# Head attention: how many of the sixteen heads VectorE divides by the softmax sums, fourteen instead of twelve

## The chip, the core and the metric

The kernel runs on one core of a Trainium2 chip. The core's engines are TensorE (PE; its weight loads are shown apart as PEld), VectorE (DVE), ScalarE (ACT), GpSimd (POOL) and SyncE (SP, which here only issues DMAs). Each engine works through its own queue in order and waits on semaphores for the others. The metric is the device time of one execution in microseconds; lower is better.

## The reference

```python
# first: x is (16, 512, 256), 16 heads of 16 channels
q = (x @ Wq.T + bq).reshape(B, S, H, D)
k = (x @ Wk.T + bk).reshape(B, S, H, D)
v = (x @ Wv.T + bv).reshape(B, S, H, D)
scores = jnp.einsum('bqnd,bknd->bnqk', q, k) / jnp.sqrt(jnp.float32(D))
attn = jax.nn.softmax(scores, axis=1)          # over the HEADS
out = jnp.einsum('bnqk,bknd->bnqd', attn, v)
x = layernorm(x + out @ Wo.T + bo)
# then: two layers of windowed attention (8 heads of 64) with rotary
# embedding, and a gated MLP; residual and layernorm behind them
...
```

The softmax runs over the sixteen heads, not over the keys: for each pair of query and key the sixteen scores are exponentiated and divided by their sum.

## The kernel before

The program has two stages, one after the other: `head_attention` (all sixteen sequences), and `layers`, which the change doesn't touch.

In head attention each of the 16 sequences (`n`) is cut into 16 **units** (`u`), one for each pair of a tile of 128 queries and a tile of 128 keys, four units to a query tile. A unit holds 128 x 128 scores for each of the 16 heads, 2048 columns on 128 partitions, in four PSUM banks (`S`). There is one set of these banks, so the score work of one unit follows that of the unit before. With u the unit in hand, the engines run this round, in this order in each queue:

- **TensorE**: subtract the maximum from the scores of u (L547, four matmuls, `less_max`, which waits for VectorE's `negmax`); sum the exponentials of u-2 into `Z` (L579, waits for GpSimd's `z4`); write the scores of u+1 (L537) bank by bank as ScalarE frees the banks; multiply the probabilities of u-3 by v (L564, `times_v`: its first half waits for VectorE's divide, its second half, heads 8 to 15, for GpSimd's as well); then pieces of the next sequence's projections, and in u = 3, 8, 11, 15 an output projection (L521, L523).
- **ScalarE**: four exponentials of u (L361); the logarithm of Z of u-2 and its inverse, once to SBUF (`zi`, L329, for GpSimd) and once to PSUM (`ZI`, L335, for VectorE); evacuations.
- **VectorE**: two reductions of the scores of u over the heads (L410; each waits for its half of the scores), their minimum `negmax` (L414); in u = 0, 4, 9, 12 the residual of a finished query tile (L421, `a_r`, which waits for L523); the **divide** of u-3 (L425); in u = 0, 4, 8, 12 `shift` (L433, `a_sh`, which waits for GpSimd's `rstd`); in u = 3, 7, 11, 15 the aggregation of the statistics (L440, L441, L443); in u = 2, 6, 10, 14 the statistics of one tile (L448).
- **GpSimd**: its part of the divide of u-3 (L269); two additions that bring 16 heads to 4 (L261, which waits for the exponentials of u, and L264); in u = 3, 7, 11, 15 `rstd` (L276).

The residual, statistics and `shift` belong to tiles finished up to ten units earlier, so those of u = 0, 4 and 8 are of the sequence before, and there are none of these in the first sequence. In the last sequence TensorE has no next sequence to project for.

The divide multiplies the exponentials in place by the inverse of the sum. The heads are split between two engines at `DVE_HEADS` (L144): VectorE takes heads 0 to `DVE_HEADS`-1 with `ZI` broadcast from PSUM, GpSimd the others with `zi` broadcast from SBUF.

```python
e = probs[uu % NE][:, :DVE_HEADS]                         # VectorE
nc.vector.tensor_tensor(e, e, ZI.unsqueeze(1).to_broadcast([P, DVE_HEADS, P]), ALU.mult).then_inc(s_p, 1)
...
e = probs[u % NE][:, DVE_HEADS:]                          # GpSimd
...
if part == 2 * (DVE_HEADS // JH):                         # TensorE, times_v; JH = 8
    pe.wait_ge(s_pp, UNITS * nn + uu + 1)
```

Of the kernel before, what the change touches and what calls it, by code (L numbers as in the profile page):

```python
# [47 lines left out]
def head_attention(nc, ctx, x_in, w, x_out, consts, W0=None, raw=None):  # L48
# [92 lines left out]
    QK_AT = ((1, 2), (4, 5), (6, 8), (9, 10))  # L141
    READY_AT = tuple(at[1] for at in QK_AT)
    PARTS = 3
    DVE_HEADS = 12  # L144
    PACK_AT = tuple(u + 2 for u in READY_AT)
    X_AT = 2
    LAST_LAG = 10
# [107 lines left out]
    def _(pool):  # L255
# [10 lines left out]
        def normalise(n, u):  # L266
            e = probs[u % NE][:, DVE_HEADS:]
            pool.wait_ge(s_zi, UNITS * n + u + 1)
            nc.gpsimd.tensor_tensor(e, e, zinv[u % 2][:].unsqueeze(1).to_broadcast([P, HEADS - DVE_HEADS, P]),  # L269
                                    ALU.mult).then_inc(s_pp, 1)  # L270
# [119 lines left out]
    def _(dve):  # L390
# [9 lines left out]
        def one(n, par, r):  # L400
            for u in units_of(n):
# [20 lines left out]
                if exists(nn):  # L422
                    dve.wait_ge(s_zp, UNITS * nn + uu + 1)
                    e = probs[uu % NE][:, :DVE_HEADS]
                    nc.vector.tensor_tensor(e, e, ZI.unsqueeze(1).to_broadcast([P, DVE_HEADS, P]),  # L425
                                            ALU.mult).then_inc(s_p, 1)
# [26 lines left out]
    def _(pe):  # L453
# [97 lines left out]
        def times_v(nn, uu, pn, part):  # L551
# [3 lines left out]
            if part == 0:  # L555
# [3 lines left out]
                if uu == 0:  # L559
                    pe.wait_ge(s_vv, 2 * nn + 2)  # L560
            if part == 2 * (DVE_HEADS // JH):
                pe.wait_ge(s_pp, UNITS * nn + uu + 1)
# [1062 lines left out]
def build(nc, w, y_out):  # L1625
    x_a = nc.dram_tensor("x_after_heads", (SEQS, SEQ, CH), F32).ap()
    x_b = nc.dram_tensor("x_after_layer", (SEQS, SEQ, CH), F32).ap()
    with ExitStack() as ctx:
        consts = make_constants(nc, ctx)
        W0 = load_layer(nc, ctx, 0)  # L1630
        raw = ctx.enter_context(nc.sbuf_tensor("raw_weights", [P, CT, 3 * INNER], F32))
        with ExitStack() as stage:
            head_attention(nc, stage, w["x"], w, x_a, consts, W0, raw)
        with ExitStack() as stage:
            W1 = load_layer(nc, stage, 1)
            layers(nc, stage, x_a, x_b, y_out, w, [W0, W1], raw, consts)
# [52 lines left out]
```

## Time and profile before

| | |
|---|---|
| three executions | 4153.17, 4155.80, 4156.33 us |
| median | 4155.8 us |
| the profiled execution | 4154.04 us, its span 4152.3 us |
| head attention within the span | about 0 to 1425 us |
| mean granted TensorE clock | 0.989 of full speed (2.4 GHz) |

The span is the profiled stretch from the first instruction to the last; some 1.7 us lie around it. The profile names an instruction by engine and source line. An idle time is shown in front of the instruction that ended it, with the instruction that released it. Matmuls are pipelined and their ends are modelled, so "PE busy" is not a proof that TensorE is at its limit.

### The profile page before, as it was taken

How to read it: one execution, taken by the hardware profiler on the slowest of the kernel's cores; microseconds unless marked ns; L12 is line 12 of the kernel's file. 1: busy time of each engine (PE TensorE's matmuls, PEld its weight loads, DVE VectorE, ACT ScalarE, POOL GpSimd, SP SyncE). 2: the span in 40 equal slices, each digit the busy share in tenths (PEclk: the TensorE clock that was granted, in tenths of full speed). 3: DMA queues.
4: the chain of work that ended last, by engine and by line, in shares of the span. 5: the costliest groups of instructions: out<-in, count | busy, mean ns of one | idle time of the engine just before them, and what ended most of it. 6: DMA issues, size and time to landing. Idle time of an engine off the chain costs nothing.

```text
span 4152.3 us, 95963 instructions
## 1 busy us (share of the span) xinstructions
PE 3909.4 (94%) x36004; PEld 3299.3 (79%) x36064; DVE 3028.8 (73%) x7348; ACT 2889.8 (70%) x7337; POOL 2171.2 (52%) x2168
## 2 busy tenths in 40 slices
PE   5999999999999689999999999999999999999997
PEld 3777777777777568888888888888888888888886
DVE  3888888888888666666666666666777777777775
ACT  3667777677766467777777777777777777777765
POOL 3999999999999623333333333323333333333332
PEclk8999999999999899999999999999999999999999
DMA  5453445445443100000000000000000000000000
GB/s 109 72 75 65 70 69 79 61 69 75 71 70 55 52 27 17 15 17 20 17 15 17 20 17 17 19 28 17 22 21 28 20 25 20 30 20 25 20 25 25
DMA packets 175106, 159.26 MB, mean 38 GB/s; under 512 B 22194, under 2 KB 173620, under 8 KB 174644
## 3 DMA queue, kind: packets, MB, share of 16 engines
q1 hardware_dynamic: 174644, 153.13, 19.6%
q8 instruction: 287, 4.70, 0.5%
q14 instruction: 175, 1.43, 0.1%
HBM read 52.40 MB, written 25.17 MB: 19 GB/s over the span
## 4 chain that ended last, share of the span: by engine, by line
PE 40%; ACT 11%; issue 8%; DVE 3%; POOL 3%; SPq 0%; DMA 0%; POOLq 0%; DVEq 0%; ACTq 0%
PE b_X L1452 11%; PE b_F L1521 5%; PE b_M L1574 5%; PE b_S L1472 4%; PE b_F L1600 4%; PE b_S L1482 3%; PE b_M L1493 3%; ACT L1180 2%; PE b_M L1565 2%; ACT L1186 2%; ACT b_hn L1095 1%; ACT b_g L1180 1%; ACT b_PT L1218 1%; DVE b_qT L1253 1%; DVE b_kT L1253 1%
## 5 line engine op out<-in xcount | busy, mean ns | idle before, releaser
L361 ACT ACTIVATE a_p<-a_S 128x512 f32<-128x512 f32 x1024 | 528.8, 603 | 225.4 <-PE a_S L547 225.4
L261 POOL TENSOR_TENSOR a_z<-a_p 128x1024 f32<-128x1024 f32 x256 | 604.6, 2362 | 106.7 <-ACT a_p L361 102.4
L1452 PE MATMUL b_X<-b_wqkv,b_hT 128*128 128x512 f32 x2304 | 648.4, 417 | 1.3 <-DVE b_hT L1288 1.3
L1521 PE MATMUL b_F<-b_hnT,b_w 128*128 128x256 f32 (+1 forms) x4224 | 584.9, 287 | 5.8 <-issue 5.8
L1212 ACT ACTIVATE b_p<-b_S,b_nb 128x256 f32<-128x256 f32 (+1 forms) x1024 | 444.6, 446 | 178.6 <-DVE b_nb L1264 178.5
L1521 PEld LDWEIGHTS b_F<-b_hnT,b_w 128*128 128x128 f32 (+1 forms) x4224 | 532.9, 187 | 18.5 <-issue 6.2
L1452 PEld LDWEIGHTS b_X<-b_wqkv,b_hT 128*128 128x128 f32 x2304 | 416.6, 190 | 99.8 <-issue 21.8
L989 POOL TENSOR_TENSOR b_t<-b_t 128x512 f32<-128x512 f32 x128 | 165.6, 1294 | 554.8 <-DVE b_t L1236 554.8
L425 DVE TENSOR_TENSOR a_p<-a_p,a_O 128x1536 f32<-128x1536 f32 x256 | 446.7, 1745 | 4.5 <-ACT a_O L335 4.0
L410 DVE TENSOR_REDUCE a_low_max<-a_S 128x128 f32<-128x1024 f32 x256 | 313.1, 1223 | 166.0 <-PE a_S L537 166.0
L1264 DVE CUSTOM_DVE_ANT_0 b_S<-b_S,b_mask,b_rn 128x256 f32<-128x256 f32 (+1 forms) x1024 | 399.8, 450 | 1.2 <-PE b_S L1472 1.2
L1218 ACT ACTIVATE b_PT<-b_S 128x1024 f32<-128x1024 f32 (+1 forms) x256 | 235.3, 919 | 211.9 <-PE b_S L1482 211.9
L1273 DVE TENSOR_SCALAR b_a<-b_F,w_b 128x256 f32<-128x256 f32 (+1 forms) x384 | 182.6, 476 | 269.9 <-ACT b_g L1123 269.8
L1600 PE MATMUL b_F<-w_w,b_a 128*128 128x256 f32 x1536 | 356.9, 382 | 10.3 <-DVE b_a L1273 5.4
L537 PE MATMUL a_S<-a_q,a_k 128*128 128x128 bf16 x4096 | 334.6, 221 | 20.1 <-DMA a_k<-a_parts 19.4
L547 PE MATMUL a_S<-a_nm,c_identr 128*128 128x512 f32 x1024 | 323.2, 437 | 25.7 <-DVE a_nm L414 25.4
L1053 POOL TENSOR_TENSOR b_rstd<-b_ve,c_half 128x1 f32<-128x1 f32 x128 | 69.9, 546 | 520.2 <-DVE b_ve L1365 520.2
L264 POOL TENSOR_TENSOR a_z<-a_z 128x512 f32<-128x512 f32 x256 | 330.8, 1292 | 20.1
L1037 POOL TENSOR_TENSOR b_hnT<-b_hnT 128x256 fp32r<-128x256 f32 x128 | 94.4, 737 | 448.2 <-ACT b_hnT L1086 448.2
L269 POOL TENSOR_TENSOR a_p<-a_p,a_zi 128x512 f32<-128x512 f32 x256 | 326.3, 1275 | 2.6 <-ACT a_zi L329 2.6
L579 PE MATMUL a_ZM<-a_z,c_ident 128*128 128x128 f32 x2048 | 325.4, 282 | 0.0
L1600 PEld LDWEIGHTS b_F<-w_w,b_a 128*128 128x128 f32 x1536 | 284.3, 191 | 48.4 <-DVE b_a L891 8.7
(154 smaller groups left out, 8888.0 us busy)
## 6 DMA issues: line engine op xcount, KB each, us to landing
a_q<-a_parts SPq DMA_DIRECT2D x256, 128.0 KB, 5.0
a_k<-a_parts SPq DMA_DIRECT2D x256, 128.0 KB, 5.0
a_x<-in_x SPq DMA_DIRECT2D x16, 512.0 KB, 4.0
a_xr<-in_x SPq DMA_DIRECT2D x64, 128.0 KB, 4.7
x_after_heads<-a_n SPq DMA_DIRECT2D x64, 128.0 KB, 2.7
b_x<-x_after_heads SPq DMA_DIRECT2D x16, 512.0 KB, 4.1
x_after_layer<-b_xo SPq DMA_DIRECT2D x32, 256.0 KB, 2.3
b_x<-x_after_layer SPq DMA_DIRECT2D x16, 512.0 KB, 4.1
```

What stands on the lines that cost most here:

```text
L261: nc.gpsimd.tensor_tensor(z8[:], e[:, 0:8], e[:, 8:16], ALU.add).then_inc(s_zt, 1)
L264: nc.gpsimd.tensor_tensor(z4[u % 4][:], z8[:, 0:4], z8[:, 4:8], ALU.add).then_inc(s_zt, 1)
L269: nc.gpsimd.tensor_tensor(e, e, zinv[u % 2][:].unsqueeze(1).to_broadcast([P, HEADS - DVE_HEADS, P]), ALU.mult).then_inc(s_pp, 1)
L361: nc.scalar.activation(probs[u % NE][:, hs], S[:, hs], ACT.Exp, scale=HDIM ** -0.5).then_inc(s_exp, 1)
L425: nc.vector.tensor_tensor(e, e, ZI.unsqueeze(1).to_broadcast([P, DVE_HEADS, P]), ALU.mult).then_inc(s_p, 1)
L537: last = nc.tensor.matmul(S[:, h], k8[:, h % JH, h // JH, kt * P:(kt + 1) * P], q8[:, h % JH, h // JH, qt * P:(qt + 1) * P], start=(h % 4 ...
L579: last = nc.tensor.matmul(Z, ident[:], z4[uu % 4][:, j], start=(j == 0), stop=(j == 3), skip_group_check=True)
L1212: last = nc.scalar.activation(probs[hf][:, i, keys(w_)], SB[:, i, keys(w_)], ACT.Exp, bias=nb[hf][:, i:i + 1], scale=-1.0, accum_out=rs[w_ ...
L1264: last = nc.vector.tensor_tensor_reduce(out=SB[:, i, cols], in0=SB[:, i, cols], in1=hidden_keys, scale=rn[w_ % 2][:, h:h + 1], scalar=LARG ...
L1452: last = nc.tensor.matmul(X[i][:], hT_of(k, a), wqkv[:, b, k, i * INNER:(i + 1) * INNER], start=(k == 0 and (a, b) == PART_PAIRS[0]), stop ...
L1521: last = nc.tensor.matmul(F[i % 2][0:size, part], w1[:, a, k, col:col + size], hnT[:, b, k, hf * 2 * P:(hf + 1) * 2 * P], start=(k == 0 an ...
L1600: last = nc.tensor.matmul(F[1][:, t], a_sb[h][:, c, t * P:(t + 1) * P], W[layer(-d)]["w2"][:, c], start=(c == 0), stop=(c == CHUNKS - 1))
```

## The change

`DVE_HEADS` goes from 12 to 14. VectorE's divide (L425) then covers 14 x 128 = 1792 columns instead of 1536, and GpSimd's (L269) 2 x 128 = 256 instead of 512, in each of the 256 units. No instruction is added, removed or moved, on any engine. TensorE's wait for GpSimd stays at the same place in `times_v`, since 12 // 8 and 14 // 8 are both 1. Buffers, DMAs and matmuls are the same.

```diff
     READY_AT = tuple(at[1] for at in QK_AT)
     PARTS = 3
-    DVE_HEADS = 12
+    DVE_HEADS = 14
     PACK_AT = tuple(u + 2 for u in READY_AT)
```

## Rows read from the trace of the kernel before

**Rows 1.** Busy by stretch: length, then busy us (instructions) per engine, clock, DMA
```profile
core 0: us, PE busy (x) PEld busy (x) DVE busy (x) ACT busy (x) POOL busy (x), PEclk, DMA share, GB/s
...
600.00:900.00 300.00, 293.21 (x3636) 235.31 (x3652) 261.19 (x315) 211.12 (x490) 284.48 (x185) 1.00 0.48 73
```

**Rows 2.** Waits from 600 to 1400 us: us in total, times, longest
```profile
DVE a_low_max L410 <- PE a_S L537: 67.0, 115, 1.5
PEld a_S L547 <- DVE a_nm L414: 57.5, 96, 1.3
...
POOL a_z L261 <- ACT a_p L361: 25.2, 53, 1.1
...
DVE a_sh L433 <- POOL a_rs L276: 4.6, 10, 0.5
```

**Rows 3.** Groups of instructions, 600 to 1400 us: busy, mean ns | idle before
```profile
L425 DVE TENSOR_TENSOR a_p<-a_p,a_O 128x1536 f32<-128x1536 f32 x152 | 265.2, 1745 | 0.3
...
L269 POOL TENSOR_TENSOR a_p<-a_p,a_zi 128x512 f32<-128x512 f32 x152 | 193.8, 1275 | 0.0
...
L421 DVE TENSOR_TENSOR a_r<-a_B,a_xr 128x256 f32<-128x256 f32 x38 | 16.2, 425 | 23.5 <-PE a_B L523 23.5
```

**Rows 4.** The page's groups: GpSimd's 256-column two-input operation
```profile
L1037 POOL TENSOR_TENSOR b_hnT<-b_hnT 128x256 fp32r<-128x256 f32 x128 | 94.4, 737 | 448.2 <-ACT b_hnT L1086 448.2
```

**Rows 5.** Timeline, unit 2 and the start of 3: start, length, instruction [idle before]
```profile
596.75 1.74 DVE L425 TENSOR_TENSOR a_p<-a_p,a_O 128x1536 f32<-128x1536 f32 x1
596.88 0.76 PEld L547 LDWEIGHTS a_S<-a_nm,c_identr 128*128 128x128 f32 x4 [0.66 <-DVE a_nm L414]
...
598.41 0.42 DVE L448 BATCH_NORM_STATS2 a_stats<-a_r 128x6 f32<-128x256 f32 x1
...
599.15 1.23 DVE L410 TENSOR_REDUCE a_low_max<-a_S 128x128 f32<-128x1024 f32 x1 [0.32 <-PE a_S L537]
```

**Rows 6.** Timeline, unit 8 (a shift, no residual)
```profile
606.79 1.74 DVE L425 TENSOR_TENSOR a_p<-a_p,a_O 128x1536 f32<-128x1536 f32 x1
606.92 0.77 PEld L547 LDWEIGHTS a_S<-a_nm,c_identr 128*128 128x128 f32 x4 [0.94 <-DVE a_nm L414]
...
608.99 0.21 DVE L433 TENSOR_SCALAR a_sh<-a_mv,a_rs 128x1 f32<-128x1 f32 x1 [0.46 <-POOL a_rs L276]
...
609.20 1.23 DVE L410 TENSOR_REDUCE a_low_max<-a_S 128x128 f32<-128x1024 f32 x1
```

**Rows 7.** Timeline, units 0 and 1 (residual, divide and shift in unit 0)
```profile
650.09 0.88 PEld L547 LDWEIGHTS a_S<-a_nm,c_identr 128*128 128x128 f32 x4
...
650.50 0.42 DVE L421 TENSOR_TENSOR a_r<-a_B,a_xr 128x256 f32<-128x256 f32 x1 [0.47 <-PE a_B L523]
650.84 1.75 DVE L425 TENSOR_TENSOR a_p<-a_p,a_O 128x1536 f32<-128x1536 f32 x1
...
652.51 0.21 DVE L433 TENSOR_SCALAR a_sh<-a_mv,a_rs 128x1 f32<-128x1 f32 x1
...
652.63 1.22 DVE L410 TENSOR_REDUCE a_low_max<-a_S 128x128 f32<-128x1024 f32 x1
...
653.25 0.81 PEld L564 LDWEIGHTS a_O<-a_p,a_v 128*32 128x32 f32 x32
...
655.02 0.29 DVE L414 TENSOR_TENSOR a_nm<-a_ZM,a_low_max 128x128 fp32r<-128x128 f32 x1
...
655.36 0.76 PEld L547 LDWEIGHTS a_S<-a_nm,c_identr 128*128 128x128 f32 x4 [0.25 <-DVE a_nm L414]
```

**Rows 8.** Timeline, units 4, 5: subtraction, reduction without idle time, next subtraction
```profile
670.95 0.87 PEld L547 LDWEIGHTS a_S<-a_nm,c_identr 128*128 128x128 f32 x4
...
673.49 1.22 DVE L410 TENSOR_REDUCE a_low_max<-a_S 128x128 f32<-128x1024 f32 x1
...
676.23 0.77 PEld L547 LDWEIGHTS a_S<-a_nm,c_identr 128*128 128x128 f32 x4 [0.60 <-DVE a_nm L414]
```

**Rows 9.** Timeline, units 12 and 13
```profile
633.34 0.29 DVE L414 TENSOR_TENSOR a_nm<-a_ZM,a_low_max 128x128 fp32r<-128x128 f32 x1
...
633.86 0.86 PEld L547 LDWEIGHTS a_S<-a_nm,c_identr 128*128 128x128 f32 x4
```

**Rows 10.** Timeline, unit 10 of the last sequence, and the drain behind unit 15
```profile
1373.88 1.22 DVE L410 TENSOR_REDUCE a_low_max<-a_S 128x128 f32<-128x1024 f32 x1
...
1376.61 0.76 PEld L547 LDWEIGHTS a_S<-a_nm,c_identr 128*128 128x128 f32 x4 [1.18 <-DVE a_nm L414]
...
1410.25 0.63 PEld L564 LDWEIGHTS a_O<-a_p,a_v 128*32 128x32 f32 x16 [1.03 <-POOL a_p L269]
...
1413.53 0.81 PEld L564 LDWEIGHTS a_O<-a_p,a_v 128*32 128x32 f32 x32 [0.48 <-DVE a_p L425]
...
1416.80 1.35 PEld L564 LDWEIGHTS a_O<-a_p,a_v 128*32 128x32 f32 x32 [2.46 <-DVE a_p L425]
```

## The prediction

> **What bounds the kernel now.** I read the busy time by stretch first. In head attention TensorE is busy 293.2 of 300 us, GpSimd 284.5, VectorE 261.2 [rows 1]. Three engines are near full, so busy shares don't say which one sets the pace, and I went on to the waits. There the reader sees a ring of two: VectorE's reductions wait for TensorE's scores 115 times, and TensorE's subtraction waits for VectorE's negmax 96 times in the same 800 us [rows 2]. Nothing on TensorE or ScalarE waits for GpSimd in that stretch: it is named as a releaser once only, of VectorE's `shift`, 10 times, 4.6 us in all. GpSimd itself is released by the exponentials 53 times [rows 2]. So GpSimd is busy beside the ring, not in it.
>
> The ring is: subtraction (L547), exponentials, scores of the next unit (L537), two reductions and a minimum on VectorE, and the next subtraction. From one subtraction to the next reduction an undisturbed unit takes 599.15 - 596.88 = 2.27 us [rows 5], and from the reduction to the next subtraction 655.36 - 652.63 = 2.73 us [rows 7]. VectorE's divide lies in the first of these legs, beside TensorE and ScalarE. It costs nothing as long as VectorE is back before the scores are there. The question is therefore, unit by unit, how much room VectorE has left before its first reduction.
>
> **The size of the edit.** VectorE's divide takes 1745 ns for 1536 columns, and its 256-column operation with one operand in PSUM 425 ns [rows 3]. The slope is (1745 - 425) / 1280 = 1.031 ns a column, so 256 more columns cost 0.264 us. The bound above is the plain share, 1745 x 256/1536 = 291 ns, which counts the fixed part twice. I take 0.264, since both rows are of the same engine, type and kind of operands; the lower bound is the same number. Over 256 units that is 68 us more VectorE busy time. GpSimd's divide falls from 1275 ns to about 737, which is what its 256-column operation takes in the second stage [rows 3, 4]: 0.54 us a unit, 138 us less busy time.
>
> **Where GpSimd's 0.54 us goes.** TensorE doesn't wait for it in steady state [rows 2], so the gain is zero there. In unit 8 VectorE's `shift` waits 0.46 us for GpSimd's rstd [rows 6]. Yet the reduction behind it starts 609.20 - 606.92 = 2.28 us after the subtraction, as in the undisturbed unit: that wait was filling room. With the longer divide it shrinks to about 0.2 us and the reduction stays where it is.
>
> **Where VectorE's 0.264 us goes**, by kind of unit:
> - *Units with statistics or aggregation* (eight of sixteen). The tightest has 0.32 us idle before its reduction [rows 5], which covers 0.264 with 0.06 left. Cost zero. If the divide grew by more than 0.32 us, that cover would be gone.
> - *Plain units, and unit 9*, have more room than those, except in the last sequence. Cost zero.
> - *Units 0, 4 and 12*, where the residual stands ahead of the divide and `shift` behind it. The residual starts when TensorE's output is there. Then residual, divide, shift and reduction follow without a gap: the reduction shows no idle time, and stands 652.63 - 650.09 = 2.54 us after the subtraction [rows 7], and 673.49 - 670.95 = 2.54 [rows 8]. That is 0.27 us later than 2.27. VectorE is already late here, so all of the 0.264 us is added to the reduction, and to the negmax.
> - *Who pays for that.* Behind unit 0 TensorE waits 0.25 us for the negmax [rows 7], behind unit 4 0.60 us [rows 8]: the whole delay passes on, and as every engine's next work hangs on that subtraction, nothing gives it back later. Behind unit 12 TensorE is busy with the projection of v. Its subtraction starts at 633.86 without an idle time, while the negmax ended at 633.63 [rows 9]; elsewhere the load follows the end of the negmax by 0.05 us (655.31 to 655.36 [rows 7]). So 0.18 us is covered, and 0 to 0.08 us is left to pay; I take 0.02, since the modelled ends of the projection hide some more room.
> - *The divide's own reader*, `times_v`, starts at 653.25 while the divide ended at 652.59 [rows 7]; 0.66 us covers 0.264.
>
> **The sum.** Units 0 and 4 have a residual in 15 sequences (not in the first): 30 x 0.264 = 7.92 us. In the last sequence TensorE projects nothing ahead, so units 12 and 9 count in full: in unit 9 the reduction also comes without idle time, and TensorE waits 1.18 us behind it [rows 10]. 2 x 0.264 = 0.53 us. Unit 12 of the other 15: 15 x 0.02 = 0.3 us (bounds 0 and 1.2). In the drain one product waits 1.03 us for GpSimd's divide, which is 0.54 us shorter, and the next two wait for VectorE's, each 0.264 longer [rows 10]: -0.54 + 0.53, nothing. Together 7.92 + 0.53 + 0.3 = 8.75 us. The second stage is untouched. On the profiled execution's 4154.04 us this gives 4162.8; that execution lies 1.8 us under the median of the three, and on the median 4155.8 it gives 4164.5 us, 0.21% slower. With the bounds of the terms the sum runs from 8.4 to 32 x 0.291 + 15 x 0.11 = 11.0 us, so 4164.2 to 4166.8.
>
> **Rivals.**
> 1. *The delay is hidden after all: 4155.8.* TensorE's busy share of 98% [rows 1] may mean that it is the pacer, the waits before L547 being ones in which earlier matmuls still drain; then 0.264 us of later negmax costs nothing. For it: the idle before the subtraction behind unit 0 is only 0.25 us [rows 7], about the delay itself. Against it: the start follows the negmax by 0.05 us, behind units 0 and 4 alike, although their other work differs.
> 2. *The cover of the statistics units fails: about 4178, slower.* The place is the 0.32 us before the reduction [rows 5]; it decides from a divide 0.32 us longer. At 0.40 us it would cost 32 x 0.40 = 12.8, the 15 units 12 another 15 x 0.22 = 3.3, and some 63 statistics units 0.08 each and 63 with aggregation a little less, 7: +23 us. Against it: even the proportional price is 0.291.
> 3. *GpSimd is in the path after all: faster, about 4147.* It is busy 95% of the time and loses 0.54 us a unit. The whole stage's waits put down to it would have to go: 17 waits for rstd like the 0.46 us one [rows 6], nearly 8 us, and a little over 1 us in the drain [rows 10], together 9 us, while rival 1 also holds so that the longer divide is free. Against it: unit 8's reduction is on time as it is. The Trainium skill, GPSIMD Engine Reference, section Engine selection, says that elementwise work on a tile belongs on VectorE and that GpSimd is about twice as slow for two inputs. The prices here agree (GpSimd (1275 - 737) / 256 = 2.1 ns a column, VectorE 1.03), and by that rule the change gives back 138 us for 68 and should be faster. It says which engine does a column cheaper, not which has room in the ring.
>
> **The numbers.** My forecast (0.2 to 0.27% slower) gets 0.71, rival 1 gets 0.17, rival 2 gets 0.06, rival 3 gets 0.06. About 0.2% (8.3 us) is what a measurement of this kernel can tell from no change, and the forecast stands almost on that line: of its 0.71 I count 0.44 above and 0.27 below. So slower 0.44 + 0.06 = 0.50, same 0.27 + 0.17 = 0.44, faster 0.06. The range 4154 to 4168 takes in the forecast with its bounds and rival 1; it leaves out rivals 2 and 3. The forecast's own range is 4162 to 4168, with the scatter of the runs.
>
> **What would show it.** In the changed kernel's profile L425 should take 2.01 us and L269 0.74. In units 0 and 4 the reduction should start 2.80 us after the subtraction instead of 2.54, and the round of sixteen units should grow by 0.53 us or a little more. The statistics units should keep about 0.06 us of idle time before L410, and `shift` in unit 8 should wait about 0.2 us. The first reduction should come without idle time in no more kinds of unit than now. GpSimd should wait for the exponentials in nearly every unit. I am wrong if L425 grows by more than 0.32 us, if TensorE's subtraction behind unit 0 keeps its place in the round, or if the round gets shorter.

## The result, and the profile after

| | median | executions |
|---|---|---|
| before | 4157.6 us | 12 |
| changed | 4166.1 us | 12 |
| ratio | 1.0021, 95% interval 1.0012 to 1.0030 | |

The changed kernel is 8.4 us slower, and the interval lies above 1. 4164.5 us was forecast, 8.7 us above the median known then; the median of before has since risen by 1.8 us with nine more executions.

The groups of instructions from 600 to 1400 us (busy, mean ns | idle before), which answer to [rows 3]:

```profile
L425 DVE TENSOR_TENSOR a_p<-a_p,a_O 128x1792 f32<-128x1792 f32 x151 | 303.6, 2011 | 0.3
...
L269 POOL TENSOR_TENSOR a_p<-a_p,a_zi 128x256 f32<-128x256 f32 x151 | 110.7, 733 | 0.0
```

VectorE's divide grew by 2011 - 1745 = 266 ns, GpSimd's fell by 542 ns. The waits of the same stretch, against [rows 2]:

```profile
POOL a_z L261 <- ACT a_p L361: 113.2, 142, 1.7
...
PEld a_S L547 <- DVE a_nm L414: 60.7, 95, 1.6
...
DVE a_low_max L410 <- PE a_S L537: 29.3, 56, 1.2
...
DVE a_sh L433 <- POOL a_rs L276: 1.9, 10, 0.2
```

GpSimd now waits for the exponentials in 142 of some 151 units, 113 us instead of 25: its saved time became idle time. VectorE's room before the first reduction fell from 67 to 29 us. TensorE waits for VectorE 3 us more. The timeline of units 0 and 1 (sequence 2, counted from 0) shows where, against [rows 7]:

```profile
231.09 0.87 PEld L547 LDWEIGHTS a_S<-a_nm,c_identr 128*128 128x128 f32 x4
...
231.84 2.01 DVE L425 TENSOR_TENSOR a_p<-a_p,a_O 128x1792 f32<-128x1792 f32 x1
...
233.77 0.21 DVE L433 TENSOR_SCALAR a_sh<-a_mv,a_rs 128x1 f32<-128x1 f32 x1
...
233.89 1.22 DVE L410 TENSOR_REDUCE a_low_max<-a_S 128x128 f32<-128x1024 f32 x1
...
236.63 0.77 PEld L547 LDWEIGHTS a_S<-a_nm,c_identr 128*128 128x128 f32 x4 [0.52 <-DVE a_nm L414]
```

From the subtraction to the reduction it takes 2.80 us (2.54 before), and TensorE's idle time behind it is 0.52 us instead of 0.25. The same point of the round comes again here:

```profile
318.78 1.22 DVE L410 TENSOR_REDUCE a_low_max<-a_S 128x128 f32<-128x1024 f32 x1
```

The round of sixteen units takes 318.78 - 233.89 = 84.89 us. In the same sequence of the kernel before it took 314.95 - 230.60 = 84.35:

```profile
230.60 1.22 DVE L410 TENSOR_REDUCE a_low_max<-a_S 128x128 f32<-128x1024 f32 x1
...
314.95 1.22 DVE L410 TENSOR_REDUCE a_low_max<-a_S 128x128 f32<-128x1024 f32 x1
```

TensorE's idle time behind unit 4 grew as well, from 0.60 us [rows 8] to 0.86:

```profile
257.75 0.77 PEld L547 LDWEIGHTS a_S<-a_nm,c_identr 128*128 128x128 f32 x4 [0.86 <-DVE a_nm L414]
```

A unit with statistics, against [rows 5]:

```profile
262.77 0.76 PEld L547 LDWEIGHTS a_S<-a_nm,c_identr 128*128 128x128 f32 x4 [0.66 <-DVE a_nm L414]
...
264.56 0.42 DVE L448 BATCH_NORM_STATS2 a_stats<-a_r 128x6 f32<-128x256 f32 x1
...
265.04 1.23 DVE L410 TENSOR_REDUCE a_low_max<-a_S 128x128 f32<-128x1024 f32 x1
```

The reduction still comes 2.27 us after the subtraction. The statistics end at 264.98, so 0.06 us of idle time is left, too little for the view to print.

Whole profiles differ in their start and in the second stage as well, so I compare the head attention stage by itself: from its first reduction to TensorE's first operation of the second stage. Of before, and below it of the changed kernel:

```profile
56.90 1.23 DVE L410 TENSOR_REDUCE a_low_max<-a_S 128x128 f32<-128x1024 f32 x1 [45.03 <-PE a_S L537]
...
1438.38 0.66 PE L1430 MATMUL b_X<-c_ident,b_x 128*128 128x128 f32 x2 [16.82 <-DMA b_x<-x_after_heads]
```

```profile
59.38 1.23 DVE L410 TENSOR_REDUCE a_low_max<-a_S 128x128 f32<-128x1024 f32 x1 [48.03 <-PE a_S L537]
...
1449.35 0.66 PE L1430 MATMUL b_X<-c_ident,b_x 128*128 128x128 f32 x2 [17.00 <-DMA b_x<-x_after_heads]
```

The stage took 1381.5 us before and 1390.0 us after: +8.5. The granted clock was 1.00 in both kernels from 600 to 1400 us. The other 3.5 us between the two spans are 2.5 us of a later first reduction and 1.0 us in the second stage, which the change doesn't touch.

### The profile page after: what moved, and what is told of

It reads as the page before. It is cut to its first block, busy times and chain, and to the rows that moved or that the text cites. A ratio compares the mean times of both kernels' runs of the same rounds, so it can differ in the third digit from the quotient of the medians.

```text
span 4164.3 us, 96023 instructions
## 1 busy us (share of the span) xinstructions
PE 3924.2 (94%) x36064; PEld 3298.5 (79%) x36064; DVE 3097.3 (74%) x7348; ACT 2886.9 (69%) x7337; POOL 2032.7 (49%) x2168
## 4 chain that ended last, share of the span: by engine, by line
PE 40%; ACT 11%; issue 8%; DVE 3%; POOL 3%; SPq 0%; DMA 0%; POOLq 0%; DVEq 0%; ACTq 0%
PE b_X L1452 11%; PE b_F L1521 5%; PE b_M L1574 5%; PE b_S L1472 4%; PE b_F L1600 4%; PE b_S L1482 3%; PE b_M L1493 3%; ACT L1180 2%; PE b_M L1565 2%; ACT L1186 2%; ACT b_hn L1095 1%; ACT b_g L1180 1%; ACT b_PT L1218 1%; DVE b_qT L1253 1%; DVE b_kT L1253 1%
## 5 line engine op out<-in xcount | busy, mean ns | idle before, releaser
L425 DVE TENSOR_TENSOR a_p<-a_p,a_O 128x1792 f32<-128x1792 f32 x256 | 514.8, 2011 | 3.6 <-ACT a_O L335 3.0
L410 DVE TENSOR_REDUCE a_low_max<-a_S 128x128 f32<-128x1024 f32 x256 | 313.1, 1223 | 114.3 <-PE a_S L537 106.6
L537 PEld LDWEIGHTS a_S<-a_q,a_k 128*128 128x128 bf16 x4096 | 274.7, 98 | 50.1 <-issue 22.8
L410 DVE TENSOR_REDUCE a_ZM<-a_S 128x128 f32<-128x1024 f32 x256 | 313.1, 1223 | 0.0
```

Source lines behind the costliest of these rows:

```text
L410: nc.vector.tensor_reduce(out=(low_max[:], HIGH_MAX)[half], in_=S[:, 8 * half:8 * half + 8].rearrange("p h q -> p q h"), axis=AX.X, op=ALU ...
L537: last = nc.tensor.matmul(S[:, h], k8[:, h % JH, h // JH, kt * P:(kt + 1) * P], q8[:, h % JH, h // JH, qt * P:(qt + 1) * P], start=(h % 4 ...
```

## The experiments

Each kernel ran against the kernel before on the same chip, eleven executions of most, twelve of the changed kernel, five of heads15 and heads11. "Stage" is the stretch just described, read from the one profile of each kernel, against 1381.5 us before. The ratio of a call is not the quotient of the two medians beside it; the two differ by up to 0.06%.

| kernel | median us | before, same call | ratio (95%) | stage us | stage against before |
|---|---|---|---|---|---|
| changed (14 heads) | 4166.1 | 4157.6 | 1.0021 (1.0012 to 1.0030) | 1390.0 | +8.5 |
| late14 | 4166.3 | 4157.0 | 1.0023 (1.0014 to 1.0032) | 1390.3 | +8.8 |
| rest14 | 4157.8 | 4157.0 | 1.0000 (0.9992 to 1.0009) | 1381.6 | +0.2 |
| swap12 | 4154.6 | 4157.0 | 0.9992 (0.9983 to 1.0001) | 1378.6 | -2.9 |
| swap14 | 4153.8 | 4157.0 | 0.9998 (0.9989 to 1.0006) | 1377.3 | -4.2 |
| heads13 | 4160.1 | 4156.7 | 1.0006 (0.9997 to 1.0015) | 1385.7 | +4.2 |
| heads15 | 4170.0 | 4156.7 | 1.0032 (1.0019 to 1.0045) | 1395.9 | +14.4 |
| heads11 | 4180.5 | 4156.7 | 1.0057 (1.0044 to 1.0069) | 1405.3 | +23.9 |
| pool_short | 4155.3 | 4156.7 | 0.9999 (0.9990 to 1.0008) | 1380.4 | -1.0 |

### Where the two heads cost: late14 and rest14

`uu` is the unit that is divided, three behind the unit in hand. late14 takes fourteen heads in the divides that run in units 0, 4, 9 and 12, rest14 in all others.

```diff
+    def dve_heads(uu):
+        return 14 if (uu + 3) % UNITS in (0, 4, 9, 12) else 12   # rest14: 12 ... else 14
...
-            e = probs[u % NE][:, DVE_HEADS:]
+            e = probs[u % NE][:, dve_heads(u):]
...
-                    e = probs[uu % NE][:, :DVE_HEADS]
+                    e = probs[uu % NE][:, :dve_heads(uu)]
```

> VectorE takes fourteen heads only in the divides that it runs in units 0, 4, 9 and 12 (behind a residual), twelve in all others: 64 of 256 divides. The ring theory (the longer divide costs only where VectorE is already late for its first reduction) expects the whole loss: 32 late reductions of 0.267 us, +8.5 us on before, about 4166. A theory of load (the price goes with the columns moved) expects a quarter of the 8.4 us, +2.1. A theory by which GpSimd's shorter divide or its traffic matters everywhere expects also about a quarter.

> The mirror image: fourteen heads in the 192 divides of the other units, twelve in units 0, 4, 9 and 12. The ring theory expects no change against before (0, within 1 us), since the statistics units' 0.32 us of room covers 0.27. The load theory expects three quarters of the loss, +6.3. If that cover were not real, each of 126 statistics and aggregation units would add something here.

A quarter of the longer divides brought the whole loss (+8.8 us in the stage), the other three quarters none (+0.2). The theory of load (the price goes with the columns moved), which expected +2.1 and +6.3, falls with both. Timelines of late14 (above) and rest14 (below), units 0 and 1 (lines are five higher here: L552 is the subtraction, L415 the reduction, L430 the divide):

```profile
226.97 0.88 PEld L552 LDWEIGHTS a_S<-a_nm,c_identr 128*128 128x128 f32 x4
...
227.73 2.01 DVE L430 TENSOR_TENSOR a_p<-a_p,a_O 128x1792 f32<-128x1792 f32 x1
...
229.78 1.21 DVE L415 TENSOR_REDUCE a_low_max<-a_S 128x128 f32<-128x1024 f32 x1
...
234.78 1.23 DVE L415 TENSOR_REDUCE a_low_max<-a_S 128x128 f32<-128x1024 f32 x1 [0.66 <-PE a_S L542]
```

```profile
224.35 0.86 PEld L552 LDWEIGHTS a_S<-a_nm,c_identr 128*128 128x128 f32 x4
...
225.11 1.74 DVE L430 TENSOR_TENSOR a_p<-a_p,a_O 128x1536 f32<-128x1536 f32 x1
...
226.90 1.22 DVE L415 TENSOR_REDUCE a_low_max<-a_S 128x128 f32<-128x1024 f32 x1
...
229.49 2.01 DVE L430 TENSOR_TENSOR a_p<-a_p,a_O 128x1792 f32<-128x1792 f32 x1
...
231.90 1.23 DVE L415 TENSOR_REDUCE a_low_max<-a_S 128x128 f32<-128x1024 f32 x1 [0.40 <-PE a_S L542]
```

In late14 the reduction comes 2.81 us after the subtraction, in rest14 2.55 as before. In rest14's unit 1 the long divide takes its 0.27 us out of VectorE's idle time, 0.40 us against the 0.66 us that late14's unit 1, with the short divide, still has.

### Taking the lateness away: swap12 and swap14

VectorE runs the divide first and the residual, which has to wait for TensorE's output, behind it:

```diff
-                if written_out(n, u, 1):
-                    ...
-                    nc.vector.tensor_tensor(resid[qt % 2][:], Y[qt], x_res[qt % 2][:], ALU.add).then_inc(s_r, 1)
                 if exists(nn):
                     dve.wait_ge(s_zp, UNITS * nn + uu + 1)
...
                                             ALU.mult).then_inc(s_p, 1)
+                if written_out(n, u, 1):
+                    ...
+                    nc.vector.tensor_tensor(resid[qt % 2][:], Y[qt], x_res[qt % 2][:], ALU.add).then_inc(s_r, 1)
```

> Twelve heads as before, but VectorE runs the divide first and the residual (which waits for TensorE's output) behind it. In units 0 and 4 the reduction should come 2.27 us after the subtraction instead of 2.54; behind unit 0 TensorE then stops waiting (0.25 us gained), behind unit 4 it gains 0.27, behind unit 12 nothing, as the projection of v hides it; in the last sequence units 9 and 12 give 0.15 and 0.27. Ring theory: 15 x 0.25 + 15 x 0.27 + 0.4 = -8.2 us on before, about 4149.5. If TensorE's own work were the pacer (the delay hidden), it expects 0.

> The same order (divide ahead of the residual) with fourteen heads. From the start of the divide at 649.95 VectorE would need 1.93 + 0.34 + 0.12 us and be ready for the reduction at about 652.34, where 652.36 is on time. Ring theory: the two heads cost nothing any more, same as swap12 within 1.5 us, about -8 us on before. If the two heads cost by their load, it is 8.4 us above swap12.

The main part of the second expectation held: with the divide first, fourteen heads cost nothing against twelve (stage 1377.3 and 1378.6 us). The round of sixteen units takes 84.17 us in both (in swap14 from 231.99 to 316.16); 1.2 of the 1.3 us between the two stages lie behind the last sequence's reduction of unit 15's scores. There TensorE waits for GpSimd's divide 0.54 and 2.19 us in swap12, and 1.83 us in swap14, whose divide on GpSimd is shorter. The same two heads cost 8.5 us in one order and none in the other. The first expectation missed, and with it the level of the second: swap12 gained 2.9 us in the stage, not 8.2, and swap14 4.2 us, not about 8. The intervals of both ratios reach past 1, so neither is shown to beat the kernel before. Both do beat the changed kernel: their intervals end at 1.0001 and 1.0006, its own begins at 1.0012. The timeline of swap12, units 4 and 5, has the reason (L419 is the divide here, L426 the residual):

```profile
250.71 0.87 PEld L547 LDWEIGHTS a_S<-a_nm,c_identr 128*128 128x128 f32 x4
251.41 2.06 ACT L361 ACTIVATE a_p<-a_S 128x512 f32<-128x512 f32 x4 [0.88 <-PE a_S L547]
...
253.08 1.23 DVE L410 TENSOR_REDUCE a_low_max<-a_S 128x128 f32<-128x1024 f32 x1 [0.22 <-PE a_S L537]
...
255.08 1.13 PE L480 MATMUL a_B<-a_xT,a_wq 128*128 128x512 f32 x2
...
255.82 0.87 PEld L547 LDWEIGHTS a_S<-a_nm,c_identr 128*128 128x128 f32 x4 [0.44 <-DVE a_nm L414]
256.53 2.06 ACT L361 ACTIVATE a_p<-a_S 128x512 f32<-128x512 f32 x4 [0.42 <-PE a_S L547]
```

First, VectorE is ready and waits 0.22 us for the scores, and they come 2.37 us after the subtraction, not 2.27: in unit 4, whose subtraction stands right behind TensorE's output projection, the exponentials begin 0.70 us after the weight load, where behind other units it is 0.59 (before: 259.20 to 259.80 in unit 6, but 248.92 to 249.62 in unit 4). VectorE was late by 0.17 us, not by 0.27. Second, an earlier negmax is of little use behind unit 4: TensorE's projection (L480) streams until 256.21, past the load at 255.82, and the exponentials again begin 0.71 us behind the load. From unit 4's subtraction to unit 6's it takes 10.24 us (250.71 to 260.95), hardly less than before (248.92 to 259.20, 10.28). The round took 316.54 - 232.37 = 84.17 us:

```profile
232.37 1.22 DVE L410 TENSOR_REDUCE a_low_max<-a_S 128x128 f32<-128x1024 f32 x1
...
316.54 1.23 DVE L410 TENSOR_REDUCE a_low_max<-a_S 128x128 f32<-128x1024 f32 x1
```

That is 0.18 us less than before, 2.7 us in fifteen rounds.

### The dose: heads13 and heads15

```diff
-    DVE_HEADS = 12
+    DVE_HEADS = 13      # heads15: 15
```

> Thirteen heads on VectorE, three on GpSimd. The ring theory expects half of what fourteen cost, 32 x 0.133 = +4.3 us on before, with the round of sixteen units 0.27 us longer (84.35 to 84.62).

> Fifteen heads on VectorE, one on GpSimd: a divide 0.40 us longer than before. If only the late units pay: 32 x 0.40 = 12.8, and 15 units 12 in which 0.28 of the 0.40 is covered, 1.8, so +13 to +15 us. If the 0.32 us of the statistics units were all the room there is (rival 2's point of decision), 63 of them add 0.08 each and 63 aggregation units 0.03, +20 to +22. Successive VectorE instructions overlap by about 0.08 us, which speaks for the first.

The stage gave +4.2, +8.5 and +14.4 us for one, two and three heads. The round of heads13 took 84.63 us (231.08 to 315.71), where 84.62 was expected. For thirteen heads the whole-kernel ratio alone could not tell the loss from none; the stage could. heads15 kept the theory's first branch. Its timeline (unit 6):

```profile
687.12 2.14 DVE L425 TENSOR_TENSOR a_p<-a_p,a_O 128x1920 f32<-128x1920 f32 x1
687.26 0.76 PEld L547 LDWEIGHTS a_S<-a_nm,c_identr 128*128 128x128 f32 x4 [0.66 <-DVE a_nm L414]
...
689.18 0.42 DVE L448 BATCH_NORM_STATS2 a_stats<-a_r 128x6 f32<-128x256 f32 x1
689.53 1.22 DVE L410 TENSOR_REDUCE a_low_max<-a_S 128x128 f32<-128x1024 f32 x1
```

This is a statistics unit. The divide is 0.40 us longer than at twelve heads, more than the 0.32 us of printed idle time, yet the reduction is on time (2.27 us after the load). It starts 0.07 us before the statistics end: VectorE begins an instruction before the last one is through, so its room is larger than the idle time printed.

### GpSimd: pool_short and heads11

pool_short leaves out part of the computation: heads 12 and 13 stay undivided.

```diff
-            e = probs[u % NE][:, DVE_HEADS:]
+            e = probs[u % NE][:, DVE_HEADS + 2:]        # pool_short
...
-    DVE_HEADS = 12
+    DVE_HEADS = 11                                      # heads11
```

> GpSimd's side of the change alone: VectorE divides twelve heads as before, GpSimd only heads 14 and 15, so that heads 12 and 13 stay undivided (this part of the computation is left out). The ring theory expects no change (0 within 1 us). If GpSimd were in the path (rival 3), the time would fall by up to 9 us.

> The other direction: eleven heads on VectorE, five on GpSimd, whose divide grows from 1.27 to about 1.54 us. VectorE's lateness alone would give a gain of a few us at most. But GpSimd's queue then needs, start to start, 2.44 + 1.25 + 1.54 us a unit and four times 0.51 for rstd, 85.7 us a round, against the 84.35 us that the round takes. So GpSimd should become the pacer: +1.4 us a round, +15 to +22 us in all, and TensorE should wait for GpSimd's divide. If GpSimd could never be the bound, the result is -4 to 0.

Cutting GpSimd's divide in half without touching VectorE's did next to nothing: ratio 0.9999, stage -1.0 us. VectorE's divide took 1744 ns in it, as before (1745), so GpSimd's shorter work doesn't speed VectorE's either. Rival 3 falls. Of the 1.0 us, 0.8 lies behind the last sequence's reduction of unit 15's scores (from there to the second stage 1399.08 to 1437.47, before 1399.21 to 1438.38). There TensorE does wait for GpSimd's divide; the wait of 1.03 us [rows 10] became this one:

```profile
1409.57 0.38 PEld L564 LDWEIGHTS a_O<-a_p,a_v 128*32 128x32 f32 x16 [0.82 <-POOL a_p L269]
```

But GpSimd was near: one head more on it cost 23.9 us in the stage, a little more than the 15 to 22 us that the length of its queue said. The timeline of heads11 shows the wait that twelve heads don't have:

```profile
676.57 2.38 POOL L261 TENSOR_TENSOR a_z<-a_p 128x1024 f32<-128x1024 f32 x1
...
679.03 1.27 POOL L264 TENSOR_TENSOR a_z<-a_z 128x512 f32<-128x512 f32 x1
...
680.26 1.55 POOL L269 TENSOR_TENSOR a_p<-a_p,a_zi 128x640 f32<-128x640 f32 x1
...
681.77 2.36 POOL L261 TENSOR_TENSOR a_z<-a_p 128x1024 f32<-128x1024 f32 x1
...
681.86 0.38 PEld L564 LDWEIGHTS a_O<-a_p,a_v 128*32 128x32 f32 x16 [0.35 <-POOL a_p L269]
```

GpSimd runs here with no gap above 0.08 us, 5.20 us from one addition to the next, and TensorE's second half of the product with v waits for its divide. The round of sixteen units took 85.81 us (235.70 to 321.51), where 85.7 was expected from the queue's length. GpSimd's late rstd holds VectorE too: in unit 8 of heads11 `shift` waits 1.32 us, and the reduction comes 2.92 us after the subtraction (275.09 to 278.01) instead of 2.27. How the 23.9 us divide between the two waits I didn't take apart.

## Why the prediction was right, step by step

- **The size of the edit.** 0.264 us was forecast from a 256-column operation of the same engine, 0.266 measured. GpSimd 0.737 forecast, 0.733 measured.
- **Which units pay.** late14 and rest14 show that the whole loss lies in units 0, 4, 9 and 12. The timelines divide it: units 0 and 4 in every round, which grew by 0.54 us (0.53 forecast), and all four in the last sequence. There it takes 77.25 us from the reduction of unit 0's scores to that of unit 15's (1333.05 to 1410.30), 76.15 before (1323.06 to 1399.21): 1.10 more, the size of four delays of 0.27. The stage grew by 8.5 us (8.75 forecast). The measured time is 8.4 us above before, 0.21%, next to the 0.2% at which the prediction had drawn its line between "same" and "slower".
- **The full delay passes on behind units 0 and 4.** TensorE's wait grew from 0.25 to 0.52 us behind unit 0 and from 0.60 to 0.86 behind unit 4. Rival 1 falls: its point, that later negmax may be free, was wrong for these two units.
- **Unit 12 costs next to nothing**, but not for the reason I gave. I took 0.02 us of the 0 to 0.08, on the ground that the modelled ends of the projection hide some more room. They hid none: the subtraction in unit 13 now follows the negmax by 0.06 us (0.23 before [rows 9]) and is 0.09 us later, 5.54 us behind that in unit 12 instead of 5.45. It comes back at once: the reduction behind unit 13's subtraction comes earlier (2.28 us after the subtraction, 2.37 before), and unit 14's subtraction follows after 5.02 us instead of 5.12. The whole round's growth is accounted for by units 0 and 4: 2 x 0.266 = 0.53. The subtractions of units 12, 13 and 14, before and below it changed:

```profile
290.73 0.86 PEld L547 LDWEIGHTS a_S<-a_nm,c_identr 128*128 128x128 f32 x4
...
296.18 0.86 PEld L547 LDWEIGHTS a_S<-a_nm,c_identr 128*128 128x128 f32 x4
...
301.30 0.76 PEld L547 LDWEIGHTS a_S<-a_nm,c_identr 128*128 128x128 f32 x4 [0.23 <-DVE a_nm L414]
```

```profile
294.30 0.86 PEld L547 LDWEIGHTS a_S<-a_nm,c_identr 128*128 128x128 f32 x4
...
299.84 0.77 PEld L547 LDWEIGHTS a_S<-a_nm,c_identr 128*128 128x128 f32 x4
...
304.86 0.76 PEld L547 LDWEIGHTS a_S<-a_nm,c_identr 128*128 128x128 f32 x4 [0.23 <-DVE a_nm L414]
```

- **The drain** was taken as nothing; from the last sequence's reduction of unit 15's scores to the second stage it took 39.05 us against 39.17.
- **The cover of the statistics units** held: 0.06 us of idle time is left, as forecast. My sign for it was badly put, though: I expected 0.06 us to be seen before L410 and no new kinds of unit without idle time. The view prints nothing so short, and so the reductions of six more units (3, 6, 7, 10, 11 and 14) show no idle time, while none stands further from its subtraction than before. The distance from the subtraction is the sign that works.
- **`shift` in unit 8** absorbed the delay: its wait for rstd went from 0.46 to 0.18 us, and the reduction stayed at 2.27 us.
- **Rival 2** stayed away, and heads15 shows that its point of decision, 0.32 us, was set too low.
- **One reading was wrong without harm.** I called VectorE 0.27 us late in units 0 and 4, by comparing with a unit without an output projection. swap12 shows 0.17 us. Where an engine is late at all and the next one waits for it, as TensorE does behind units 0 and 4, a further delay counts in full however late it was, so the forecast of a slowdown didn't depend on it; the forecast of a gain in swap12 did, and missed by 5 us.

## What to carry to other kernels

In a ring of engines, moving work is priced unit by unit: free where the receiving engine still waits for its input, at full price where it is already late and the engine behind it waits for it, and worth nothing on the engine that gives it up if nobody waited for that one. Read lateness as the distance from the event that starts the leg, compared within the same kind of unit, since printed idle times leave out short gaps and overlaps. A delay is passed on in full where the next engine waits for it, but an advance is only worth the distance to the next thing that would be late, so a gain needs that one looked up first.

## What the runs showed that I had not expected

- The start of an execution scatters by nearly as much as the whole effect of the change: the first reduction came at 53.2 us in the profile of rest14 and at 60.3 us in that of heads11, 7.1 us later, both waiting for the first scores. What scatters ahead of them I didn't look for. The stage from one trace each put heads13 4.2 us above before, where medians of eleven and 21 executions did not tell the two apart.
- The limits on the two sides lie close: with twelve heads VectorE's lateness costs 2.9 us (what swap12 gained) and GpSimd's length about 1 (pool_short); one head more on GpSimd cost 24 us, one more on VectorE 4 us.
- An idle time on TensorE's weight load is not an idle array: in swap12 the load waited 0.44 us for VectorE while a projection was still streaming for 0.39 us after the load began. That end is modelled; what speaks for it is that the exponentials came 0.71 us behind the load, not 0.59.
